# Values as the second projection panel, filler turns at the start, and a new order of late statistics and gate in a decoder layer on one core

## The reference

```python
x = x + attn(layernorm(x), Wq, Wk, Wv, Wo)   # 32 heads of queries, 8 of keys and values, rotation, causal softmax
x = x + matmul(fake_quant(layernorm(x)), fake_quant(ctx))
x = x + experts(layernorm(x))                # router of rank 16, top 16 of 64 experts, rank 8 each
```

## Time and profile before

| stretch, us | what | TensorE busy, us | granted clock, mean |
|---|---|---|---|
| 0 to 97 | head, panel 0, start of panel 1 | 71.43 | 0.98 |
| 97 to 1144 | panels 1 to 3, attention, product with Wo | 1035.20 | 1.00 |
| of it 784 to 895 | units 56 to 63 and the last reads | 103.84 | 0.97 |
| 1144 to 1217 | quantised product and experts, tiles 0 and 1 | 63.28 | 0.95 |
| 1217 to 1320.8 | tiles 2 to 7 | 99.26 | 1.00 |
| all | span 1320.8; the profiled execution took 1322.61 | 1269.2 | 0.992 |

### The profile page before, as it was taken

How to read it: one execution, slowest core, us unless ns; L and a number is a source line. 1 busy time by engine, 2 the same in 40 slices (tenths; PEclk the granted TensorE clock), 3 DMA queues, 4 the chain that set the end, 5 groups by cost and what they waited for, 6 DMA issues and landing times. The chain is left out here.

```text
span 1320.8 us, 19919 instructions
## 1 busy us (share of the span) xinstructions
PE 1269.2 (96%) x7025; PEld 1091.4 (83%) x7025; DVE 818.0 (62%) x1798; ACT 770.2 (58%) x1582; POOL 602.1 (46%) x446
## 2 busy tenths in 40 slices
PE   5879999999999999999999999999999999988998
PEld 5758998888888888888888888888888887766887
DVE  7788224555555555555555655655787788777663
ACT  4411137777767767777777867863333355555540
POOL 4665666777767777687667745420000000020100
PEclk9999999999999999999999998999999999999999
DMA  7033134646849659477386578758964486100001
GB/s 270 17 120 120 65 123 149 184 128 191 232 127 237 195 142 275 134 172 207 93 232 168 133 214 262 210 187 256 283 197 132 151 287 200 58 1 17 33 33 48
DMA packets 117122, 207.42 MB, mean 157 GB/s; under 512 B 10128, under 2 KB 51088, under 8 KB 113440
## 3 DMA queue, kind: packets, MB, share of 16 engines
q1 hardware_dynamic: 112992, 176.79, 40.7%
q0 software_dynamic: 4032, 29.36, 12.0%
HBM read 147.40 MB, written 88.08 MB: 178 GB/s over the span
## 5 line engine op out<-in xcount | busy, mean ns | idle before, releaser
L1235 DVE TENSOR_TENSOR pT_lo<-banks,pT_hi 128x512 fp32r<-128x512 f32 (+1 forms) x192 | 103.7, 595 | 179.2 <-ACT pT_hi L970 179.1
L1634 PE MATMUL banks<-ob_hi,oa_hi 128*128 128x512 f32 x384 | 149.7, 390 | 0.9 <-DVE ob_lo L1272 0.9
L1634 PE MATMUL banks<-ob_hi,oa_lo 128*128 128x512 f32 x384 | 149.6, 390 | 0.0
L1634 PE MATMUL banks<-ob_lo,oa_hi 128*128 128x512 f32 x384 | 149.6, 389 | 0.0
L1592 PE MATMUL banks<-xc,nring_hi_a 128*128 128x512 f32 x448 | 140.2, 394 | 1.2 <-DVE q_made L1185 1.2
L1592 PE MATMUL banks<-xc,nring_hi_b 128*128 128x512 f32 x448 | 139.9, 394 | 0.0
L954 ACT CAST oa_hi<-oraw 128x1024 fp32r<-128x1024 f32 x48 | 50.5, 1052 | 142.7 <-PE banks L1634 133.1
L970 ACT CAST pT_hi<-banks 128x512 fp32r<-128x512 f32 (+1 forms) x192 | 86.5, 526 | 75.9 <-PE banks L1562 75.8
L1833 POOL TENSOR_TENSOR resid<-resid,colterm 128x1024 f32<-128x1024 f32 x8 | 19.1, 2382 | 223.7 <-ACT colterm L1891 137.6
L1244 DVE CUSTOM_DVE_ANT_0 prob<-banks,mask 128x512 f32<-128x512 f32 (+3 forms) x256 | 109.8, 485 | 0.3 <-DVE resid L1163 0.3
L728 POOL TENSOR_TENSOR q_lo<-q_raw,q_hi 128x512 fp32r<-128x512 f32 x64 | 86.7, 1356 | 40.7 <-ACT q_hi L907 40.6
(11 more groups left out here) (245 smaller groups left out, 3450.4 us busy)
## 6 DMA issues: line engine op xcount, KB each, us to landing
q_raw<-qk_dram SPq DMA_DIRECT2D x64, 256.0 KB, 4.1
o_S<-o_st SPq DMA_DIRECT2D x64, 256.0 KB, 3.9
w<-in_L_attn_Wo SPq DMA_DIRECT2D x32, 512.0 KB, 5.4
oraw<-o_S SPq DMA_DIRECT2D x32, 512.0 KB, 3.8
nraw<-in_L_attn_Wq SPq DMA_DIRECT2D x28, 512.0 KB, 5.5
o_S<-o_S POOLq DMA_DIRECT2D x12, 1024.0 KB, 10.0
o_S<-o_N POOLq DMA_DIRECT2D x12, 1024.0 KB, 10.2
resid<-in_x SPq DMA_DIRECT2D x16, 512.0 KB, 7.7
```

What stands on the lines that cost most here:

```text
L1235: nc.vector.tensor_tensor(pT[1][:, sl], turned_chunk(turned, mixed, c), as32(pT[0][:, sl]), ALU.subtract).then_inc(pT_lo, 1)
L1634: ins = nc.tensor.matmul(step_bank(m, t), oa[a][:, s % 2, k, t * P:(t + 1) * P], ob[c][:, s % 2, k, :], start=(q == 0 and k == 0 and i == ...
```

## The change

Panels: `TURNED` is now (0, 2), so that panel 1 makes the first half of the values, and panel 2 the queries; panel 2's `alpha` lies in banks 6 and 7. VectorE's order in panels 0 and 1 is written anew: the two C00 tiles of panel 1 come early, the C01 sums ahead of the rotations of C11, and the copies of panel 1 among the rotations.

Head: TensorE turns the identity 72 times ahead of the first fill. The four t1 go from VectorE to GpSimd, behind weight sum S3, and the low half of the fifth weight product waits for t2 instead of t1; t2 no longer waits for a weight.

Attention: unit 55 gets one product instead of two, so the last one moves to place 0 of unit 56, with its reads, its rotation and its stores.

Last stage: late_stats(4) and (5) go into earlier places on VectorE, late_scale(0) ahead of gate(0) and scale_of(2) behind it; the square root for them goes ahead of root(1) on ScalarE, the copies of turned tiles 3 and 4 to other places; TensorE turns quantised tiles 2 and 3 earlier; the two halves of `add_out` stand on both sides of the low halves of the next tile.

```diff
--- before.py
+++ after.py
@@ -35,7 +35,7 @@
-PANELS, TURNED = 4, 2
+PANELS, TURNED = 4, (0, 2)
@@ -52,6 +52,9 @@
+
+WARM = 72
@@ -74,7 +77,7 @@
 PLACES = [(1, 1)] + [(u, p) for u in range(2, UNITS)
-                     for p in ((0, 1, 2) if u in (3, 5, 8, 12, 16) else (0,) if u in (50, 52) else (0, 1))]
+                     for p in ((0, 1, 2) if u in (3, 5, 8, 12, 16) else (0,) if u in (50, 52, 55) else (0, 1))]
@@ -313,7 +316,7 @@
     def alpha(s, fb):
-        return banks[:, (6 if s % 2 and s != LASTP else 0) + fb, :]
+        return banks[:, (6 if s in (1, 2) else 0) + fb, :]
...
@@ -469,11 +472,11 @@
             sp.wait_ge(made, n + 1)
-            if s < TURNED:
+            if s in TURNED:
...
             else:
-                f0 = (s - TURNED) * 512 + i * 256
+                f0 = s // 2 * 512 + i * 256
@@ -616,7 +619,7 @@
                 load_q(u + 2)
-            if u == LAST_JOB_UNIT + 1:
+            if u == LAST_JOB_UNIT:
@@ -708,6 +711,10 @@
+        def t1(t):
+            pool.wait_ge(t3_sum, TPB)
+            nc.gpsimd.tensor_tensor(right(t, 0), right(t, 0), left(t, 0), ALU.subtract).then_inc(t_sum, 1)
@@ -800,8 +807,11 @@
         w_low(3)
-        pool.wait_ge(t_sum, TPB)
+        pool.wait_ge(ln_out_v, 5)
         weight_sum(0, "S3")
+        for t in range(TPB):
+            t1(t)
+        pool.wait_ge(t_sum, 2 * TPB)
@@ -826,7 +836,7 @@
         for u in range(UNITS):
-            if (u - 1, 0) in JOB_AT:
+            if (u - 1, 0) in JOB_AT and u - 1 < LAST_JOB_UNIT:
@@ -837,6 +847,8 @@
                 narrow_low(j)
+            if u == LAST_JOB_UNIT:
+                turn_added(JOBS - 1)
@@ -1103,13 +1115,8 @@
-        def t1(t):
-            dve.wait_ge(t3_sum, t + 1)
-            nc.vector.tensor_tensor(right(t, 0), right(t, 0), left(t, 0), ALU.subtract).then_inc(t_sum, 1)
-
         def t2(t):
-            dve.wait_ge(t_sum, t + 1)
-            dve.wait_ge(w_lo, 5)
+            dve.wait_ge(t_sum, TPB + t)
...
@@ -1138,14 +1145,14 @@
             dve.wait_ge(p1_read, 2 * s + fb + 1)
-            if s >= 1:
+            if s >= 2 or s == 1 and which == 3:
...
             dve.wait_ge(p_done, done(s, "P4", fb))
-            if s < TURNED:
+            if s in TURNED:
...
@@ -1164,19 +1171,26 @@
-        def c11_turns(s):
-            for fb in range(2):
-                dve.wait_ge(c11_read, 2 * s + fb + 1)
-                rope(alpha(s, fb), tile_no(s, "C11", fb))
+        def c11_turn(s, fb):
+            dve.wait_ge(c11_read, 2 * s + fb + 1)
+            rope(alpha(s, fb), tile_no(s, "C11", fb))
+
+        def c01_sum(s, fb):
+            dve.wait_ge(p_done, done(s, "P3", fb))
+            dve.wait_ge(u_read, 4 * s + fb + 1)
+            link(nc.vector.tensor_tensor(gamma(s, fb), gamma(s, fb), u_copy(s, 2, fb), ALU.add))
+
+        def c01_turn(s, fb):
+            rope(gamma(s, fb), tile_no(s, "C01", fb))
...
             n = tile_no(s, "C01", fb)
-            dve.wait_ge(p_done, done(s, "P3", fb))
-            dve.wait_ge(u_read, 4 * s + fb + 1)
-            if s < TURNED:
-                link(nc.vector.tensor_tensor(gamma(s, fb), gamma(s, fb), u_copy(s, 2, fb), ALU.add))
-                rope(gamma(s, fb), n)
+            if s in TURNED:
+                c01_sum(s, fb)
+                c01_turn(s, fb)
             else:
+                dve.wait_ge(p_done, done(s, "P3", fb))
+                dve.wait_ge(u_read, 4 * s + fb + 1)
@@ -1356,8 +1370,6 @@
             t3(t)
-        for t in range(TPB):
-            t1(t)
@@ -1368,36 +1380,42 @@
         keep_u(0, 2, 0)
+        c00(1, 0)
         keep_u(0, 2, 1)
+        c00(1, 1)
...
         c11(0, 1)
-        c00(1, 0)
-        c00(1, 1)
...
         c10(0, 1)
-        c11_turns(0)
-        c01(0, 0)
+        c01_sum(0, 0)
+        c11_turn(0, 0)
+        c01_sum(0, 1)
         keep_u(1, 2, 0)
-        c01(0, 1)
+        c11_turn(0, 1)
         keep_u(1, 2, 1)
+        c01_turn(0, 0)
+        keep_u(1, 3, 0)
+        c01_turn(0, 1)
+        keep_u(1, 3, 1)
...
                 keep_u(s, 2, 1)
-            keep_u(s, 3, 0)
-            keep_u(s, 3, 1)
+                keep_u(s, 3, 0)
+                keep_u(s, 3, 1)
...
             c11(s, 1)
-            if s < TURNED:
-                c11_turns(s)
+            if s in TURNED:
+                c11_turn(s, 0)
+                c11_turn(s, 1)
@@ -1499,9 +1517,9 @@
                 if p == "P1" and s == LASTP:
-                    pe.wait_ge(made, tile_no(s - 1, "C00", fb) + 1)
-                elif p == "P1" and s >= 2:
-                    pe.wait_ge(made, tile_no(s - 2, "C11", fb) + 1)
+                    pe.wait_ge(made, tile_no(0, "C11", fb) + 1)
+                elif p == "P1" and s == 2:
+                    pe.wait_ge(made, tile_no(1, "C00", fb) + 1)
...
@@ -1636,6 +1654,8 @@
+        for n in range(WARM):
+            nc.tensor.transpose(banks[:, 7, 0:P], ident[:], ident[:])
@@ -1922,14 +1942,14 @@
         highs("b", range(2))
+        late_root(0)
...
         highs("b", range(4, 6))
+        copy_turned(3)
         root(2)
-        copy_turned(3)
-        late_root(0)
@@ -1945,11 +1965,11 @@
                 root(i + AHEAD)
-            if i == 1:
-                copy_turned(i + 3)
...
                 highs("x", (2 * i + 2, 2 * i + 3))
+            if i == 1:
+                copy_turned(i + 3)
@@ -2040,12 +2060,11 @@
-        def add_out(t):
-            for half in range(2):
-                sl = slice(half * 512, half * 512 + 512)
-                n = PB["out", 2 * t + half]
-                dve.wait_ge(p_done, n + 1)
-                nc.vector.tensor_tensor(resid[:, t, sl], pb[n % 2], resid[:, t, sl], ALU.add).then_inc(o_added, 1)
+        def add_out(t, half):
+            sl = slice(half * 512, half * 512 + 512)
+            n = PB["out", 2 * t + half]
+            dve.wait_ge(p_done, n + 1)
+            nc.vector.tensor_tensor(resid[:, t, sl], pb[n % 2], resid[:, t, sl], ALU.add).then_inc(o_added, 1)
@@ -2056,6 +2075,7 @@
         row_term(0)
+        late_stats(TPB)
@@ -2071,6 +2091,7 @@
         lows("x", range(2))
+        late_stats(TPB + 1)
@@ -2079,14 +2100,12 @@
         add_product(2)
+        lows("b", range(4, 6))
         product_stats(2)
-        lows("b", range(4, 6))
+        late_scale(0)
+        gate(0)
         scale_of(2)
-        late_stats(TPB)
-        late_stats(TPB + 1)
-        gate(0)
         lows("x", (2, 3))
-        late_scale(0)
@@ -2103,14 +2122,16 @@
             gate(i)
+            add_out(i - 1, 0)
...
                 lows("x", (2 * i + 2, 2 * i + 3))
-            add_out(i - 1)
+            add_out(i - 1, 1)
...
         low("z", TT - 1)
-        add_out(TT - 1)
+        add_out(TT - 1, 0)
+        add_out(TT - 1, 1)
@@ -2230,8 +2251,9 @@
         router_matrix()
-        turn_fills("a", range(5, 8))
+        turn_fills("a", range(5, 7))
         turn_quantised(2)
+        turn_fill("a", 7)
@@ -2248,11 +2270,12 @@
                 turn_fills("b", range(4, 6))
+                turn_quantised(3)
...
                 expand(i - 1, (0,))
-            if i + 3 < TT:
+            if 1 <= i < TT - 3:
```

More of the change, by code:

```diff
@@ L459, in load_w @@
         def load_w(s, names):
-            W, col = (Wk, 0) if s == 0 else (Wq, 0) if s < TURNED else (Wv, s - TURNED)
+            W, col = (Wk, 0) if s == 0 else (Wq, 0) if s in TURNED else (Wv, s // 2)
             for name in names:
@@ L1165, in c11 @@
                 dve.sem_inc(made, 1)
-        def c11_turns(s):
-            for fb in range(2):
-                dve.wait_ge(c11_read, 2 * s + fb + 1)
-                rope(alpha(s, fb), tile_no(s, "C11", fb))
+        def c11_turn(s, fb):
[7 more added lines that the diff above has]
+            rope(gamma(s, fb), tile_no(s, "C01", fb))
         def c01(s, fb):
             n = tile_no(s, "C01", fb)
-            dve.wait_ge(p_done, done(s, "P3", fb))
-            dve.wait_ge(u_read, 4 * s + fb + 1)
-            if s < TURNED:
-                link(nc.vector.tensor_tensor(gamma(s, fb), gamma(s, fb), u_copy(s, 2, fb), ALU.add))
-                rope(gamma(s, fb), n)
-            else:
+            if s in TURNED:
+                c01_sum(s, fb)
+                c01_turn(s, fb)
+            else:
+                dve.wait_ge(p_done, done(s, "P3", fb))
+                dve.wait_ge(u_read, 4 * s + fb + 1)
                 slot_free(n)
@@ L1517, in product @@
                 dst = product_bank(s, p, fb)
-                for tt in ((None,) if s < TURNED else (2 * fb, 2 * fb + 1)):
+                for tt in ((None,) if s in TURNED else (2 * fb, 2 * fb + 1)):
                     for k in range(KH):
```

## The result

The changed kernel takes 1300.41 us (median of 4 runs, 1299.56 to 1303.54), the kernel before 1322.62 in runs beside it: a ratio of 0.9837, 95% interval 0.9813 to 0.9861. The forecast of 1303.5 lies between 3.1 and 1.2 us above, inside its range, and the sign was right. The two profiled executions, with spans of 1298.4 and 1301.7 us, stood at 0.999 and 0.997 of full clock, that of before at 0.992. Of the eight executions of the changed kernel the three at 0.997 took 1303.10 to 1303.54 us, the five at 0.999 took 1299.56 to 1301.52: most of its spread goes with the clock.

What follows compares the result with a forecast made beforehand. TensorE, busy 1269.2 of 1320.8 us, was taken as the bound, so only its idle and slow time could be won. Head 12.5, moved product 1.5 and last stage 5.1 sum to 19.1, giving 1303.5 us, own range 1300 to 1307.

Steps and rivals of the forecast that it cites:

- Head, up to P6: Start to product P6 of panel 0: 2.6 us gained, from fillers and t1 on GpSimd, less longer value products.
- fillers: Identity turns ahead of the first fill: TensorE's pace doubles earlier, gain 1.2 us (bounds -1.8 and 1.9).
- The value products' 0.3: Four value half-products ahead of P6 of panel 0, each 0.13 us longer: 0.3 us of it not hidden.
- Panel 1: P6 of panel 0 to panel 1's end: 59.5 us becomes 51.3, gain 8.2, a 0.4 wait replacing earlier waits and half clock.
- Panel 2 and behind: Panel 2 with queries runs at 5.52 us per product instead of 5.76: 1.7 us gained.
- slower: Rival: panel 2's rotations run into panel 3 and the attention behind it, say 1330 us; chance 0.03.
- The moved product: Product moved from unit 55 to 56: 1.5 us gained (bounds -1 and 4), with new short waits in units 57 and 58.
- The last stage: Gate and late statistics: hidden(1) 2.0 us earlier, the 3.12 us wait at 1214.63 gone; sum 5.1 (bounds 2 and 7).
- VectorE stays the bound: Rival in panel 1: waits move to its P4 and P5, four of 0.9 give 1307 us; chance 0.12.
- the head doesn't follow: Rival: port and GpSimd chain keep P6 where it was and the filler is idle, 1306.1 us; chance 0.12.
- the tail only reorders: Rival in the last stage: the 3.12 wait stays, perhaps 2.0 too, 1306.6 to 1308.6 us; chance 0.13.
- The clock comes along: Rival: thinner waits bring no half clock at units 56 and 58, once less in the tail, 1299.2 us; chance 0.12.

Runs made afterwards that it cites:

- e6: The changed kernel without the 72 turns of the identity (WARM = 0), all else kept: 1303.76 us (4 runs).
- e5: The changed kernel measured again without any edit: 1302.31 us (4 runs) against 1321.99 for the kernel before, ratio 0.9856.
- e8: The changed kernel with queries as panel 1 and values as panels 2 and 3 again, VectorE's new order kept: 1302.79 us (one run).
- e1: The kernel before with the head's part alone (72 identity turns, t1 on GpSimd, t2 without the weight wait): 1319.11 us, ratio 0.9977.
- e7: The changed kernel with VectorE's old order of blocks in panels 0 and 1, values still as panel 1: 1306.55 us (one run).
- e3: The kernel before with only its last narrow product moved to place 0 of unit 56: 1321.97 us (10 runs), ratio 1.000.
- e2: The kernel before with the panels' part alone (values as panel 1, queries as panel 2, VectorE's new order): 1312.60 us, ratio 0.9925.
- e4: The kernel before with the last stage's part alone: 1318.35 us (10 runs), ratio 0.9973.
- e10: The changed kernel with both halves of add_out behind the low halves of the next tile's x, as before: 1301.43 us (one run).
- e9: The changed kernel with ScalarE copying turned tile 4 ahead of the exponentials of tile 1 again: 1302.76 us (one run).
- e11: The changed kernel with three orders changed (ScalarE's P6 weights, GpSimd's first-step low half, VectorE's low halves ahead of scale_of(2)): 1300.32 us, ratio 0.9837.

## Why the prediction was right, and where not

**Head, up to P6.** 2.6 forecast, 2.66 to 2.98 measured (0.3 of the larger because the first tile came earlier, at 13.39). Counted from the first turn of data it is 2.61 and 2.64. Of its pieces: fillers 1.2, measured 1.2, the least of the 1.2 to 1.9 above, since the pace doubled early in the execution of before too (5.56 us from the first turn to P1). The rest 1.4, measured 1.4 (45.58 us from the first turn to P6 in e6, 46.98 before). The value products' 0.3 is there too: 44.37 us in e5, 44.09 in e8, which has none ahead of P6. That moving t1 does the 1.4 is not tested by a run of its own; e1 has it together with the fillers. The fillers' schedule is not fixed. In e5 the pace doubled some 4 us in and they ended at 12.51, as forecast (4.2 us, 12.6), with 1.17 us to spare. In the first execution it doubled between 8 and 9 and they ended at 13.48, with nothing to spare. The first tile wasn't held up: it was turned 0.86 after VectorE began to normalise it in both (12.53 to 13.39, 12.82 to 13.68). TensorE by the microsecond, same columns as above, first execution and e5:

```profile
7.00:8.00 1.00, 1.00 (x7) 1.00 (x6) 0.76 (x3) 0.00 (x0) 0.00 (x0) 1.00 1.01 389
8.00:9.00 1.00, 1.00 (x9) 1.00 (x9) 1.00 (x2) 0.00 (x0) 0.00 (x0) 1.00 1.07 382
```

```profile
6.00:7.00 1.00, 1.00 (x9) 1.00 (x8) 0.96 (x2) 0.00 (x0) 0.00 (x0) 1.00 1.01 401
7.00:8.00 1.00, 1.00 (x12) 1.00 (x11) 0.53 (x2) 0.00 (x0) 0.00 (x0) 1.00 0.99 368
```

t3 was lengthened by 0.66 beside S3, as the row on the blocked 4-element operation had it; the Trainium skill's rule ("SBUF — State Buffer", the shared port pair) agrees. The wait of 1.40 for GpSimd stayed (1.39).

**Panel 1.** 8.2 forecast, 8.65 measured; the 0.4 of wait that I put in did not come: the last copy of panel 1 was done 36.3 us behind P6 (57.73 to 93.99), where I had 36.9. The number was right, the account behind it only half: I let the gain rest on VectorE having one operation in place of four or five. By e7 and e8 that alone leaves 3.5 us of wait, and the order alone leaves 0.4. The sum worked because it counted the new order's work behind the sums C10 and never asked what the old number of rotations would do in that order. The piece that carries most is the order: putting it back costs 5.0 us (e7), putting the queries back 1.2 (e8).

**Panel 2 and behind.** 1.7 forecast, 2.1 to 2.2 measured: a turned product takes 38.13 / 7 = 5.45 there, not the 5.52 read from panel 0, which was busy time with the end of the last matmul in it (from start to start it was 21.89 / 4 = 5.47). This gain is no saving of work: the five value products that panel 1 has there now take 28.91 / 5 = 5.78 each, and with the 0.3 ahead of P6 give back 1.9 of it, as the forecast had counted. No wait in panel 3: the rival "slower" had no hold.

**The moved product.** 1.5 forecast, 1.75 to 2.25 in the traces, 0.1 +/- 1.6 by the runs of e3. That the traces come near is partly luck of the one execution of before, which had two stretches at half clock. The fourth row of the table takes 641.75 to 642.60 us in e1, e2 and e4 (old place, one stretch), and 640.80 to 641.74 in seven of the eight executions with the new place and this order (after, e3, e5, e7 to e10), 642.62 in e6: about 1 us. The wait ahead of unit 55's turns was 1.25, not 1.5 to 2. Those forecast behind it (about 1.3, 1.0, 1.1 and 0.8) were 2.1, 1.6 and 0.7 in e5, and the fourth, of 1.4, lay at a later step; at step 2 e5 was 1.06 ahead, 1.1 forecast. The rest of the gain in those units is clock: with 9.2 us of waits e5 is 1.75 us faster than before with 7.7. By e1, e2 and e4 the second stretch of before was worth 0.9 to 1.75; I had taken "about half of 3.4", and let only part of it into the sum.

**The last stage.** 5.1 forecast; 6.3 at full clock, 3.9 with 6.8 us at half clock. Where the stretch is 3.4 long, gate, `hidden(1)` and `multiply(4)` give 5.0: that was the case in the forecast ("the half clock behind them" stays). The account held in both pieces: `hidden(1)` starts 1.7 us earlier than the stages before it explain (81.36 us behind 1096.24 against 83.05 behind 1112.21; 2.0 forecast), and the 3.12 is gone through ScalarE's order (e9). Which of the moves of the late statistics, the gate and the turns gives the 1.7 was not taken apart. That add_out was split did nothing.

**Rivals.** "VectorE stays the bound", "the head doesn't follow" and "the tail only reorders" are out: the changed kernel has no wait in panel 1, e1 moves P6 to 57.75, and e9 brings the wait at `multiply(4)` back. "The clock comes along", 1299.2 at a chance of 0.12, comes near the first execution (1300.17, span 1298.4), though its one stretch lies where this rival had none, in unit 57; the forecast's own 1301.7 is the span of the second. It was wrong to treat this as a question about the change: the clock differs from execution to execution, and the median lies between.

## What to carry to other kernels

When an engine is late for a consumer, first look for the idle time that it has ahead of the jam, and move work there; only then take work off it. A copy that waits for another engine, put ahead of a table load and a short urgent operation, delays all three: let the urgent one go first. Before an order is changed to end a wait, look which chain ends next behind it, and compare short waits over several executions, since a stretch at half clock moves one of them by more than most edits. One profiled execution of the kernel before made the moved product look worth 2 us; three others with the old place put it at some 1.

## What the runs showed of the hardware

- The half clock after short idle times is not a fixed property of a kernel. With the same two waits (1.9 and 1.5 us) TensorE went on at 2.4 GHz (changed kernel, e9), or fell to 1.2 GHz for 3.4 us (e4, e6, e7, e8, e10) or 6.8 us (e5). The cost in the last stage was 1.35 to 1.5 us for the short one, 2.45 for the long one. The Trainium skill ("TensorE: Matmul & The Clock Gate", Part 1) says that the number of slow matmuls in one kernel differs between runs; these traces agree, for the middle of a kernel too.
- Half clock just ahead of a wait can be nearly free. In the changed kernel 3.4 us of it lay on the first step (783.2 to 786.6), and the wait of 1.58 us for the probabilities that e5 shows there was absent. The fourth row of the table took 641.24 us, and 641.53 in e9 with the same stretch; four executions without one (e5, e7, e8, e10) took 641.17 to 641.74. It isn't a rule: e6, whose stretch began 0.7 us later behind unit 0, took 642.62.
- VectorE and GpSimd slowed one another when each had an operation on SBUF. In e11 the rotation ran beside VectorE's low half:

```profile
778.34 1.47 DVE L1274 TENSOR_TENSOR ob_lo<-w,ob_hi 128x1024 fp32r<-128x1024 f32 x1 [1.85 <-ACT ob_hi L952]
778.68 2.27 POOL L771 TENSOR_TENSOR n_sin<-q_made,n_sin 128x512 f32<-128x512 f32 x1
780.91 1.28 POOL L772 TENSOR_TENSOR n_u<-n_u,q_made 128x512 f32<-128x512 f32 x1
```

  2.27 instead of 1.28, and 1.47 where 1.22 is usual for that low half. The rotation ended 1.14 us behind the low half (780.95 and 779.81), so little of it can have run beside it.
